# Where the list of further units is waited for, and when layer 1 makes it

## The reference, cut to what matters

```
x = x + attention(layer_norm(x))
t = layer_norm(x)
logits = t @ router.T                    # 256 x 8
top 2 experts of each token, weights from a softmax
layer 0:  h = silu(t @ gate[e].T) * (t @ up[e].T) @ down[e].T     # hidden sizes 432 to 1584
layer 1:  h = relu(t @ w1[e].T + b1[e]) @ w2[e].T + b2[e]         # hidden size 768
x = x + t + sum over the two experts of weight * h
```

## Time and profile before

| | |
|---|---|
| time, median of 3 runs | 215.62 us (215.5 to 216.11) |
| the profiled execution's own time | 214.29 us |
| its span, first to last instruction | 212.5 us |
| PE busy | 189.1 us (89%) |
| DVE / ACT / POOL busy | 99.9 / 63.3 / 32.0 us |
| mean granted TensorE clock | 0.964 |

### The profile page before, as it was taken

How to read it: one execution, slowest core, us unless ns; L and a number is a source line. 1 busy time by engine, 2 the same in 40 slices (tenths; PEclk the granted TensorE clock), 3 DMA queues, 4 the chain that set the end, 5 groups by cost and what they waited for, 6 DMA issues and landing times.

```text
span 212.5 us, 4269 instructions
## 1 busy us (share of the span) xinstructions
PE 189.1 (89%) x1656; PEld 130.0 (61%) x1656; DVE 99.9 (47%) x302; ACT 63.3 (30%) x144; POOL 32.0 (15%) x65
## 2 busy tenths in 40 slices
PE   7899899998969999999999688888996999990992
PEld 7679777567426656765558577555862567570471
DVE  0342787747732222354313239785695474440131
ACT  2243587627112222231132245883320000000000
POOL 1413400001891000000000012000139300000000
PEclk9999999999979999999999999999998899997698
DMA  6999999995000019999301999991000899996001
GB/s 211 425 437 409 414 457 401 432 384 181 21 3 0 0 29 364 401 420 424 147 3 24 350 405 414 427 419 54 0 3 0 270 369 352 356 355 231 0 3 45
DMA packets 7388, 51.21 MB, mean 241 GB/s; under 512 B 888, under 2 KB 2368, under 8 KB 3136
## 3 DMA queue, kind: packets, MB, share of 16 engines
q1 hardware_dynamic: 6784, 50.05, 59.8%
q10 hardware_dynamic: 576, 0.79, 1.2%
HBM read 50.64 MB, written 0.20 MB: 239 GB/s over the span
## 4 chain that ended last, share of the span: by engine, by line
PE 70%; DMA 11%; DVE 9%; issue 5%; ACT 3%; SPq 1%; POOL 1%; DVEq 0%; POOLq 0%
PE bank L1375 10%; DMA w<-bias_rows_dram 9%; PE bank L1454 7%; PE bank L1196 5%; PE bank L1078 5%; PE bank L1402 4%; PE bank L1151 4%; PE bank L1441 3%; PE bank L1330 3%; PE bank L1359 3%; PE bank L1208 3%; PE bank L1415 3%; PE bank L1110 3%; PE bank L1180 3%; PE bank L1309 2%
## 5 line engine op out<-in xcount | busy, mean ns | idle before, releaser
L1375 PE MATMUL bank<-w,scratch 128*64 128x512 f32 (+3 forms) x112 | 23.3, 547 | 3.1 <-DVE job_regs L939 3.1
L1078 PE MATMUL bank<-ones 128*128 128x128 f32 x162 | 23.6, 299 | 2.0 <-POOL ones L526 1.4
L1078 PEld LDWEIGHTS bank<-ones 128*128 128x128 f32 x162 | 21.7, 210 | 2.9 <-POOL ones L526 1.4
L685 ACT ACTIVATE scratch<-bank,neg_max 128x256 f32<-128x256 f32 x48 | 19.7, 480 | 7.8 <-DVE neg_max L810 7.6
L1454 PE MATMUL bank<-w,scratch 128*64 128x192 f32 x216 | 20.2, 332 | 0.0
L1454 PEld LDWEIGHTS bank<-w,scratch 128*64 128x64 f32 x216 | 14.4, 136 | 9.1 <-issue 4.8
L576 POOL TENSOR_SCALAR scratch<-const,place,gate 128x64 f32<-128x64 f32 x32 | 18.0, 579 | 5.4 <-issue 5.4
L534 POOL TENSOR_TENSOR rstd<-var_eps,minus_half 128x2 f32<-128x2 f32 x4 | 2.8, 710 | 101.5 <-DVE var_eps L747 101.5
L1196 PE MATMUL bank<-const,scratch 128*128 128x128 f32 x96 | 15.1, 284 | 2.5 <-ACT scratch L685 1.2
L810 DVE TENSOR_REDUCE neg_max<-bank 128x2 f32<-128x512 f32 x24 | 15.7, 681 | 3.2 <-PE bank L1180 3.2
L614 ACT ACTIVATE scratch<-bank 128x384 f32<-128x384 f32 x6 | 2.9, 491 | 44.3 <-PE bank L1424 44.3
(11 more groups left out here) (175 smaller groups left out, 280.9 us busy)
## 6 DMA issues: line engine op xcount, KB each, us to landing
w<-experts_dram SPq DMA_DIRECT2D x16, 1152.0 KB, 14.4
w<-items_dram SPq DMA_DIRECT2D x8, 1152.0 KB, 8.2
w<-experts_dram SPq DMA_DIRECT2D x1, 3624.0 KB, 13.7
w<-experts_dram SPq DMA_DIRECT2D x1, 3024.0 KB, 30.9
w<-experts_dram SPq DMA_DIRECT2D x1, 2496.0 KB, 20.1
w<-experts_dram SPq DMA_DIRECT2D x1, 2016.0 KB, 24.4
w<-experts_dram SPq DMA_DIRECT2D x1, 1704.0 KB, 40.2
w<-bias_slots_dram SPq DMA_DIRECT2D x1, 1536.0 KB
```

The costliest lines, as they stand in the source:

```text
L685: nc.scalar.activation(probs[:, h % HB, t, :], bank[h % HB][:, t * TOK:(t + 1) * TOK], ACT.Exp, bias=neg_max[:, h, t:t + 1]).then_inc(prob ...
L1078: nc.tensor.matmul(bank[b][:, 0:P], ones[:], ones[:], start=True, stop=True)
L1375: nc.tensor.matmul(first_bank(m, which)[rows, to:to + wide], xe_hi[:, e], w0[:, at:at + wide], start=col == 0, stop=False, tile_position=( ...
```

## The change: what it does

Layer 0: PE's wait for `jobs_ready` moves from the end of iteration m = 0 to iteration m = 1, ahead of `down(0)`. Layer 1: the whole list is moved ahead. DVE counts right after chosen and makes the columns after xn_lo, both ahead of the gates; PE's two list matmuls stand in the middle of the gathering and the third at its end, ahead of the transpose of the gates; the wait for `jobs_ready` stands in m = 1 ahead of `turn_hidden(0)`. In both layers the gathering runs the `xn_hi` matmuls of both halves first and then the `xn_lo` ones, and the count takes two DVE instructions where it took four.

```
 def count_candidates(layer):                                   # DVE
-    step(nc.vector.tensor_copy(count[:], bank[4][:, TT * E:(TT + 1) * E]))
-    step(nc.vector.tensor_tensor(cand_count[:, 0:E], count[:], cand[:, 0:E], ALU.mult))
-    step(nc.vector.tensor_reduce(cand_count[:, E:E + 1], cand_count[:, 0:E], AX_X, ALU.add))
-    nc.vector.tensor_tensor(cand_there, cand_count[:, E:E + 1], cand[:, E:E + 1], ALU.is_gt).then_inc(sems["cand_ready"], 1)
+    step(nc.vector.scalar_tensor_tensor(cand_count, bank[4][:, TT * E:(TT + 1) * E], cand[:, E:E + 1], cand[:, 0:E],
+                                        ALU.is_gt, ALU.mult))
+    nc.vector.tensor_reduce(cand_there, cand_count, AX_X, ALU.add).then_inc(sems["cand_ready"], 1)
...
 def experts(layer):                                            # DVE
+    if layer == 1:
+        count_candidates(1)
     nc.vector.tensor_tensor(xn_lo, xn[:], xn_hi.bitcast(F32), ALU.subtract).then_inc(xn_split, 1)
+    if layer == 1:
+        list_slots(1)
     gates(layer)
-    count_candidates(layer)
+    if layer == 0:
+        count_candidates(0)
+    else:
+        number_macros(1)
     dve.wait_ge(xe_psum, 2 * layer + 2)
     nc.vector.tensor_copy(xe_lo.rearrange("p e s -> p (e s)"), bank[3][:]).then_inc(xe_vec, 1)
     if layer == 1:
+        number_slots(1)
         dve.wait_ge(combT_psum, 1)
...
-    list_slots(layer)
+    else:
+        list_slots(0)
+        number_macros(0)
     iteration(layer, 0)
-    number_slots(layer)
+    if layer == 0:
+        number_slots(0)
...
 def iteration(layer, m, prepared=None):                        # PE
     first_upper(layer, m)
-    if m == 0:
-        pe.wait_ge(sems["cand_ready"], 1)
...
+    if m == 0 and layer == 0:
+        number_candidates(0)
+    if m == 1 and layer == 1:
+        pe.wait_ge(sems["jobs_ready"], 1)
+    if m > 0:
         turn_hidden(layer, m - 1)
...
     first_lower(layer, m)
-    if m == 0:
-        pe.wait_ge(sems["slots_ready"], 3)
...
+    if m == 0 and layer == 0:
+        sum_slots(0)
+    if m == 1 and layer == 0:
         pe.wait_ge(sems["jobs_ready"], 1)
-    else:
+    if m > 0:
         down(layer, m - 1)
...
 def experts(layer):                                            # PE
     for c in range(2):
-        gather(bank[2 + c][:], c, lambda t: chosen[:, t].rearrange("p e s -> p (e s)"), TT * layer).then_inc(xe_psum, 1)
+        for t in range(TT):
+            pe.wait_ge(chosen_ready, TT * layer + t + 1)
+            nc.tensor.matmul(bank[2 + c][:], xn_hi[:, t, c * P:(c + 1) * P], chosen[:, t].rearrange("p e s -> p (e s)"),
+                             start=t == 0, stop=False)
     if layer == 1:
+        number_candidates(1)
+    pe.wait_ge(xn_split, layer + 1)
+    for c in range(2):
+        for t in range(TT):
+            last = nc.tensor.matmul(bank[2 + c][:], xn_lo[:, t, c * P:(c + 1) * P], chosen[:, t].rearrange("p e s -> p (e s)"),
+                                    start=False, stop=t == TT - 1)
+        last.then_inc(xe_psum, 1)
+    if layer == 1:
+        sum_slots(1)
```

More of the change, by code:

```diff
@@ L205, in metaformer_kernel @@
         slot_of = carve_xnT(3 * items).rearrange("p (a k) -> p a k", a=3)
-        cand_count, cand_there, cand_at, job_steps, job_number = (carve_xnT(n) for n in (E + 1, 1, 2, max(JOB_MACROS), 1))
+        cand_count, cand_there, cand_at, job_steps, job_number = (carve_xnT(n) for n in (E, 1, 2, max(JOB_MACROS), 1))
         cand_of = carve_xnT(3)
@@ L914, in count_candidates @@
                 sems, cand = main[layer], candidates[:, layer]
-                step(nc.vector.tensor_copy(count[:], bank[4][:, TT * E:(TT + 1) * E]))
-                step(nc.vector.tensor_tensor(cand_count[:, 0:E], count[:], cand[:, 0:E], ALU.mult))
-                step(nc.vector.tensor_reduce(cand_count[:, E:E + 1], cand_count[:, 0:E], AX_X, ALU.add))
-                nc.vector.tensor_tensor(cand_there, cand_count[:, E:E + 1], cand[:, E:E + 1], ALU.is_gt).then_inc(sems["cand_ready"], 1)
-                dve.wait_ge(sems["cand_ready"], 1)
-                step(nc.vector.tensor_scalar(cand_of, cand[:, E + 1:E + 4], cand_there, None, ALU.mult))
+                step(nc.vector.scalar_tensor_tensor(cand_count, bank[4][:, TT * E:(TT + 1) * E], cand[:, E:E + 1], cand[:, 0:E],
+                                                    ALU.is_gt, ALU.mult))
+                nc.vector.tensor_reduce(cand_there, cand_count, AX_X, ALU.add).then_inc(sems["cand_ready"], 1)
             def list_slots(layer):
                 sems, n = main[layer], ITEMS[layer]
+                dve.wait_ge(sems["cand_ready"], 1)
+                done = tick(nc.vector.tensor_scalar(cand_of, candidates[:, layer, E + 1:E + 4], cand_there, None, ALU.mult))
                 dve.wait_ge(sems["cand_psum"], 1)
+                dve.wait_ge(vec_step, done)
                 step(nc.vector.tensor_scalar(cand_at, bank[6][:, 0:2], 1.0, None, ALU.add))
@@ L929, in list_slots, with number_macros @@
                                             ALU.is_equal, ALU.mult).then_inc(sems["slots_ready"], 1)
+            def number_macros(layer):
                 step(nc.vector.tensor_scalar(job_steps, const[:, C_STEPS:CONST_W], cand_at[:, 1:2], None, ALU.is_lt))
@@ L1299, in places_of, with gather @@
                 keep_clock(KEEP_PLACE)
-            def gather(out_ap, c, tokens, ready=None):
+            def gather(out_ap, c, tokens):
                 for i, part in enumerate((xn_hi, xn_lo)):
                     for t in range(TT):
[L1305 to L1308, removed]
                         last = nc.tensor.matmul(out_ap, part[:, t, c * P:(c + 1) * P], tokens(t),
@@ L1467, in gather_job, with number_candidates, sum_slots @@
                 last.then_inc(sems["job_gathered"], 1)
+            def number_candidates(layer):
+                sems = main[layer]
+                pe.wait_ge(sems["cand_ready"], 1)
+                nc.tensor.matmul(bank[6][:, 0:1], upper, cand_there, start=True, stop=True, skip_group_check=True)
+                nc.tensor.matmul(bank[6][:, 1:2], ones[:], cand_there, start=False, stop=True, skip_group_check=True).then_inc(sems["cand_psum"], 1)
+            def sum_slots(layer):
+                sems, n = main[layer], ITEMS[layer]
+                pe.wait_ge(sems["slots_ready"], 3)
+                out_ap = bank[6][:, 0:3 * n].rearrange("p (a k) -> p a k", a=3)
+                nc.tensor.matmul(out_ap, ones[:], cand_slots[:, :, 0:n], start=True, stop=True).then_inc(sems["slots_psum"], 1)
             def iteration(layer, m, prepared=None):
```

6 lines of the change are left out of this document (removed).

## The result

The changed kernel takes **209.97 us** (median of four runs, 209.33 to 210.51); the kernel before took 215.56 beside it. The ratio is 0.974, with an interval of 0.970 to 0.978. The forecast was 209.8. The profiled execution took 210.15 us itself, over a span of 208.3. Now and then an execution of any of these kernels takes over 1.5% longer than the fastest of the same kernel; the ratios leave those out, the medians in us do not.

What follows compares the result with a forecast made beforehand. PE was taken to bound layer 0 from first_upper(1) on, and the units' DMA stream, started by the list, layer 1. Gains of 3.12 and 2.7 us make 5.8, so 215.62 becomes 209.8 us, range 208.6 to 211.6.

Steps and rivals of the forecast that it cites:

- Layer 0, 3.12 us: Layer 0's experts: moving PE's wait gains 3.34 us, less 0.22 for the new gathering; bounds 1.31 and 3.34.
- the idle of 1.53: Layer 0, PE ahead of first_upper(1): waiting for the list, released by DVE's line 939; its 1.53 us go.
- The overrun of 0.22: Layer 0's new gathering: xn_hi matmuls run past xn_lo's arrival, making first_upper(0) 0.22 us late; bounds 0 and 0.55.
- The covers: Layer 0: slack of 0.9 us at turn_hidden(0) and 2 us at the moved wait, so both cost nothing.
- the clock's 1.81: Layer 0, first_upper(1): at full clock its eight passes take about 1.73 us instead of 3.54, 1.81 off.
- Layer 1, 2.7 us: Layer 1's list: job_regs written at 160.70 to 160.78 instead of 163.44, 2.7 us earlier; bounds 1.9 and 3.1.
- The gates and POOL: Layer 1: gates at 159.0 not 157.26, POOL's weighted at 159.2 not 157.43; PE still 3.2 us ahead at turn_hidden(0).
- The stream moves as one: Layer 1's unit loads: first issue moves from 164.84 to 162.1, the end to 193.7, the tail follows unchanged.
- The 32 us that were to prove the step wrong: Layer 1's stream: the forecast counts as wrong if it takes longer than 32 us; 31.6 expected.
- The clock did not fall anyway: Rival, layer 0: the clock falls despite the moved wait, total gain 4.0, 211.6 us; chance 0.08.
- The stream's end did follow its start: Rival, layer 1: something other than its start sets the stream's end, only layer 0 gains, 212.5 us; chance 0.06.
- The slow clock through layer 0's start: Rival, layer 0: clock falls in the reordered gathering, staying half until the first down; 217.6 us, chance 0.03.

Runs made afterwards that it cites:

- moved alone: The kernel before with only layer 0's wait for jobs_ready moved ahead of down(0) in m = 1: 212.38 us, ratio 0.986.
- biases by PE: The changed kernel with layer 1's further units' biases added by PE selection matmuls, bias rows loaded once: 205.02 us, ratio 0.953.
- filling the wait: Six small matmuls in layer 0's wait: kernel before, ratios 1.000 and 1.003; kernel with PE-made biases and wait at end of m = 0, 0.960.

## Why the prediction was right

**The places.** Layer 0's wait and layer 1's stream were named as the two things that bound, and each alone moved the time. Both experiments that undo one of them give back some of the gain.

**Layer 0, 3.12 us.** At the place: from `place` to `turn_hidden(0)` 12.85 us before and 9.65 after, 3.20 less. Of the terms, the idle of 1.53 went but for 0.17 ahead of the third list matmul. The burst took 1.86 up to `turn_hidden(0)`, not 1.73, and before it had taken 3.48: 1.62 off, not 1.81. The overrun of 0.22 in the new gathering wasn't there: old and new gathering give 9.64 and 9.65. The misses roughly cancel. The covers held: `turn_hidden(0)` follows the burst without a wait, and `job_regs` is long written when `down(0)` asks for it.

**How much of it arrives.** By the times the moved wait is worth 0.0138 x 215.6 = 3.0 us (moved alone), 2.0 (biases by PE), and only 0.7 to 1.8 where the changed kernel has it put back (0.983 against 0.979 and 0.974); by the profiles 2.7. So 3.12 was some 0.4 too much by the profiles, and the part to doubt is the clock's 1.81: filling the wait won 1.3 and 1.6 at the place and 0.7 to 0.8 at the next `place`, and in the time between a loss of 0.6 and a gain of 0.6 (ratios 1.003 and 1.000, and 0.963 to 0.960). That the clock's half arrives in the time is not shown, and the reason isn't settled. The burst in m = 1 had the full clock in all eight profiles with the moved wait, but falls came at other places, with and without the edit; whether one avoided makes another likelier, these runs can't tell. That eight matmuls of layer 0's attention took 2.08 us in one profile of the changed kernel and 1.16 in the other agrees with what the Trainium skill says (TensorE: Matmul & The Clock Gate, section "Part 1: The HAM clock gate"), that the point at which the clock changes differs between runs of one kernel.

**Layer 1, 2.7 us.** `job_regs` ends 6.18 us behind `place` (158.82), where it ended 8.98 behind it (163.44): 2.80 nearer. The first issue is 2.81 nearer. The gates and POOL did come later, and PE made it good, as worked out: `turn_hidden(0)` at 161.16 doesn't wait.

**The stream moves as one.** Yes in its start; its length isn't as fixed as the step took it. In this profile it took 32.4 us (160.21 to 192.64) instead of 31.6, so that its end won 1.95 instead of 2.81; PE's idle was 6.60. In the second profile of the same kernel the idle was 5.74, against 5.8 forecast. The 32 us that were to prove the step wrong were drawn too narrowly: over the profiles the stream took 31.6 to 32.8.

**The sum.** Own time 210.15 in this profile, 208.5 forecast. The 1.65 are the fall in layer 0's attention (1.00), layer 0 (2.82 from `place` to `place`, not 3.12: 0.30) and layer 1 (2.38 from `place` to the end, not 2.7: 0.32). Over several profiles 2.7 and 2.9 to 3.2 make 5.6 to 5.9 us, where 5.6 was measured, and 5.0 on the second chip (215.31 to 210.28). That 209.8 came within 0.2 us of the measured 209.97 is in part luck: layer 0 was taken some 0.4 too large and layer 1 0.2 to 0.5 too small, and the ratio's interval alone spans 209.1 to 210.8 us.

**The rivals.** The clock did not fall anyway in m = 1. The stream's end did follow its start, with the list late or early. The slow clock through layer 0's start didn't come.

## What to carry to other kernels

Move a wait to the first instruction that would spoil what it protects, and make a list that starts a long transfer as early as its inputs allow: but price the second by the transfer's end, for the early list was worth about half a microsecond in the profiles, and nothing that the times could tell, once PE and not the stream set layer 1's end. Look at the rate of a stream and not only at its busy row; here the rate's dips were worth more than the whole change. A half clock behind a wait is a true cost of the profile at hand, and still a poor one to count in full, since another execution may have it elsewhere.

## What the runs showed of the hardware

- Small loads into 32 partitions, between loads of 1152 KB, held up the stream far beyond their bytes: 9.44 MB alone took some 24 us (393 to 459 GB/s in the full slices of the view), with 0.78 MB more 32 us, the engines busy all the time. What exactly makes them dear wasn't tried.
- The clock can fall or not behind the same idle: 1.54 us of idling was followed by a burst of 2.83 us in one profile and of 1.51 in another.
- A matmul that sums over 8 rows is no cheaper per column than one over 128: in the kernel with the biases by PE, four of 8x384 took 1.55 us (1536 columns), and four of 128x192 (768 columns) 0.82 in the same timeline.
